# Setup of an eight-batch gated cross-attention kernel taken apart: loads in order of need on two queues, whole fills of ones, constants as steps of the first batch, later weights in the loop

## The chip, the cores and the metric

The kernel runs on one core of a Trainium2 chip. The metric is the device time of one execution in microseconds (us), lower is better. Engines: PE multiplies matrices, DVE, ACT and POOL work on vectors, SP only issues transfers (DMA). Each engine runs its own list of instructions in order and waits on semaphores that others raise. DMAs are issued by an engine's queue and flow on 16 shared DMA engines.

## The reference

Input x is 8 batches of 256 rows by 128 features, with a context of the same shape. Four layers follow each other. Each adds, behind a tanh gate, an attention with 16 heads of 8 features (queries from the layer-normed x, keys and values from the context), and then, behind another gate, a feed-forward part of the layer-normed x:

```python
x = x + tanh(g_xattn[l]) * attention_l(layernorm(x), ctx, ctx)
x = x + tanh(g_ffn[l]) * ffn_l(layernorm(x))
```

Layer 2's attention is causal, layer 3's keeps for each head only the 51 queries of 256 that lie best on the keys. The feed-forward parts: layer 0 routes 3 rows in 4 through a 128x128 block with gelu; layer 1 is a mixture of 8 experts (best 2 of 8) plus a shared one, with silu; layer 2 the same with hidden width 512 and gelu; layer 3 rounds x and the weight w3 to a six-bit grid in blocks of 32 and multiplies them.

## The kernel before, in words

The work of one batch is a fixed list of some 260 small steps (`stream_steps`, L73): `keys`, `stats`, `norm`, `turn`, `query`, `maxima` (scores and their row maxima), `max_parts`, `max_turn`, `attend` and `weigh` (scores again, turned, exponential, product with the values), `heads`, `project`, and the feed-forward steps. Four batches are in flight in four slots; batch b + 4 takes the slot of batch b. In which order the batches take turns is written out by hand as digits in `TURNS_TAKEN` (L120); `SCHEDULE` (L152) is the resulting list of 2144 (step, batch, layer, part). Every engine walks the same list and issues its own part of each step, so its queue has the order of the list, and an engine that waits in one step holds back all later ones. `signals` (L155) tells how often each step raises which semaphore, and the wait values are counted from it.

Scores come from stacked tiles: `k_st` and `q_st` hold, for each pair of heads, keys and queries split into three bf16 terms. ACT writes the first term (L573) and a copy (L578), POOL makes the other two (L517 to L522), and SP scatters them with six DMAs per `keys` (L468) and six per `query` (L477) into every eighth row of the stack. One row in 32 of `k_st` holds ones and the same row of `q_st` the negated row maxima, which `max_turn` moves there by one SP DMA of 16 KB (L481); PE's first `attend` of that batch and layer waits for it (L789). After the last `attend`, `max_clear` (L485) copies a row of zeros of `k_st` over the maxima.

Before the loop stands the setup:

- SP (L434 to L447) issues w3, then the 14 `attention_loads` (L385), then context and x of four slots.
- DVE (L882 to L970) clears slot 0 (`clear`, L416: `q_st` to zero, two small fills, `k_st` to zero), writes the rows of ones one by one (`set_ones`, L423), quantises w3 in 14 parts (`fp6`, L898), waits for all attention loads, makes bf16 and gated copies of constants, splits the weights of all layers (L953), and at last fills `junk` and raises `setup_done` (L970).
- POOL (L499 to L508) clears slots 1 to 3, writes their twelve rows of ones (L426), issues six `ffn_loads` and seven `big_loads` (two of 2 MB each), and waits for `setup_done`.
- ACT (L552 to L556) and PE (L641 to L645) wait for the loads, turn the quantised w3, and wait for `setup_done`.

In the loop, POOL's `norm` makes h (L527, L531) and behind it, for the attention norms, adds the gated output bias `gbo` to x (L539), which raises `xb_ready`; SP's next load of x and DVE's `project` wait for that.

Of the kernel before, what the change touches and what calls it, by code (L numbers as in the profile page):

```python
# [12 lines left out]
P = 128  # L13
# [16 lines left out]
CBANKS = 2  # L30
VR = HD + 1
# [41 lines left out]
def stream_steps():  # L73
# [6 lines left out]
    for l in range(LAYERS):  # L80
        out += norm(l) + [("turn", l, 0), ("query", l, 0)] + [("load_x", 0, 0)] * (l == 0)
# [5 lines left out]
        out += tiles + [("max_parts", l, 0), ("max_parts", l, 1), ("max_turn", l, 0)]  # L87
# [33 lines left out]
0000101011033112132200302000000201301213101001001001001120201200200210021121031211210312021312030011  # L121
0131231231010122101220101000212020122003223023311030221111122132131312122223010030320122333203323032
0230230310323212303203103200010320123103100103100001313332003230103031032011331011121121021123032220
0120000001110102023223213210231112012023223213212312201213113102230212011320032011112002110002321013
2201222222311332112101221331230303102321230300020322232302210013022013203100033103011310302130012131
2112113021031322213011233301100211020221010223301220312211100120203022103030212000103030110110210032
1230002213301223303021111222002220311023300322101220013131001102123211312113022222013222100201001302
3111021012023021201202202132203020212103311333010120000010000120031301000133001010103010203032220332
3010302231332300013211202110111233113313111220212101111101313101301320103131022031031132303313030000
0323310222112210203414141122113222112131341142421133122214152534343545234534345522432422344323332254  # L130
5523453542445445245424542534523434342343543544523345424245443523553543534445355544354425435245534243
2533453425235342332325532353232256655565563453545663444454434636453536456336433644346436443364333646
4563445345436353465446653364363336453666433434636635466366534436543653666346475474477464446566575646
4564676456546547645566457575755765767554757575754754546767476545476457547764767765746556576555775756
5556755566577557665555756746656747564574646744466746656677775764656664654475446757456776654666666574
4666446766756664566645756666546647557557567567575577745547554447465746477677677644776776675644447547
5654756566745475567455677576747656467665775474474476576475477477466464574777476746774557754477757477
5446475766545666555766647547546564754765647576667765556654746554575664566447566476574474747747747767
6447475764765445567544455676554565465655556757764447774476754556464776465744455757457677747576775774
7755775466746657667677776657766746754647664677765455557455455767455564666546666646645664665466757667  # L140
7767567564765756777776757466764677745757774575747574775757746767577757677757567776757647675456767676
76746464767747576767675675767467675674476677
# [12 lines left out]
def signals(step, b, l, part):  # L155
# [3 lines left out]
        "load_x": {},  # L159
        "load_ctx": {},  # L160
# [5 lines left out]
        "norm": {f"h_ready{s}": 1, "xb_ready": int(l < LAYERS or l == 2 * LAYERS - 1)},  # L166
# [7 lines left out]
        "max_parts": {"m_parts_done": part},  # L174
# [92 lines left out]
def flamingo(nc, x, ctxT, attn_w, bias_cols, bias_rows, g_all, router0, block0, router1, fc1, fc2,  # L267
             gate_up, down, router2, w1, ws1, b1_cols, w2, ws2, b2_all, w3, ident_in, causal_qk,
             causal_kq, before_in, iota_in, out):
    with ExitStack() as ctx:  # L270
# [10 lines left out]
        def sem(name):  # L281
# [92 lines left out]
        w3_loaded, cleared, attn_loaded, ffn_loaded, big_loaded = sem("w3_loaded"), sem("cleared"), sem("attn_loaded"), sem("ffn_loaded"), sem("big_loaded")  # L374
        zeroed_first, zeroed = sem("zeroed_first"), sem("zeroed")
        gates_done, w3_quantised, w3_turned = sem("gates_done"), sem("w3_quantised"), sem("w3_turned")
        w3_copied, setup_done, setup_step = sem("w3_copied"), sem("setup_done"), sem("setup_step")
# [7 lines left out]
        attention_loads = [  # L385
            (wqk_in.rearrange("d l j n -> d l (j n)"), attn_w[:, :, 0:2, :].rearrange("d l j n -> d l (j n)")),
            (wvo[:, :, :, :].rearrange("d l j n -> d l (j n)"), attn_w[:, :, 2:4, :].rearrange("d l j n -> d l (j n)")),
            (bcol[0:HALF, :, :], bias_cols.rearrange("(m a) l c -> a m l c", a=2)[0, :, :, :]),
            (bcol[HALF:P, :, :], bias_cols.rearrange("(m a) l c -> a m l c", a=2)[1, :, :, :]),
            (ident[:, :], ident_in), (bv_all[:, :], bias_rows[:, R_BV:R_BO].broadcast_to([P, LAYERS * D])),  # L390
            (rows_in, bias_rows[:, R_BO:R_GB].broadcast_to([P, R_GB - R_BO])),
            (gate_b[:, :], bias_rows[:, R_GB:R_GB + EXPERTS].broadcast_to([P, EXPERTS])), (gates[:, :], g_all.broadcast_to([P, 2 * LAYERS])),
            (cqk, causal_qk), (ckq, causal_kq), (iota[:, :], iota_in),
            (before_f, before_in), (r0_sb[:, :], router0)]
# [983 lines left out]
```

## Time and profile before

| | us |
|---|---|
| median of 3 runs | 1045.1 (1043.42 to 1047.93) |
| profiled execution | 1045.38, its span 1043.6 |
| busy PE / DVE / ACT / POOL | 920.3 / 784.0 / 608.0 / 407.3 |
| mean granted PE clock | 0.954 |

The span runs from the first instruction to the last; the execution's own time is 1.8 us longer. Busy time is the sum of the durations of an engine's instructions; what lies between is idle. `A <-B` behind a row names what ended an idle time.

### The profile page before, as it was taken

To read this page: it belongs to the slowest core of one execution; us is meant where nothing else is said; L and a number is where in the kernel's file an instruction comes from. 1 tells how busy PE (TensorE), PEld (TensorE's weight loads), DVE (VectorE), ACT (ScalarE), POOL (GpSimd) and SP (SyncE) were. 2 spreads that over 40 slices of the span, in tenths; PEclk is the share of its full clock that TensorE was granted. 3 is DMA by queue.
4 is the path that set the end of the run, shared out by engine and by line. 5 is a ranking of instruction groups with operands and counts; after the bars stand their busy time and mean duration, and the time that the engine had idled before them with its cause. 6 is when DMAs were issued, how large, how long until landed. Compare 5 with 4: busy or idle time off the path is not lost.

```text
span 1043.6 us, 22358 instructions
## 1 busy us (share of the span) xinstructions
PE 920.3 (88%) x7921; PEld 606.1 (58%) x7921; DVE 784.0 (75%) x2688; ACT 608.0 (58%) x1301; POOL 407.3 (39%) x481
## 2 busy tenths in 40 slices
PE   0379789999999999889986799999999999999883
PEld 0224345665589888357633355556469987767522
DVE  7289999887655455997898999888946456656787
ACT  0147667445675544778674575655685457786641
POOL 9812533224244113464346144333460333252322
PEclk9769999999999999999998899999999999999956
DMA  6921211101010000002112111111010010010000
GB/s 182 283 62 30 57 35 33 32 17 46 6 43 21 17 16 17 19 23 53 26 28 60 26 37 49 33 33 32 19 48 2 17 32 16 3 32 1 19 2 22
DMA packets 67037, 39.91 MB, mean 38 GB/s; under 512 B 7911, under 2 KB 64768, under 8 KB 66928
## 3 DMA queue, kind: packets, MB, share of 16 engines
q1 hardware_dynamic: 65008, 31.70, 11.9%
q0 software_dynamic: 1920, 6.78, 2.1%
q8 instruction: 66, 1.08, 0.5%
q14 instruction: 43, 0.35, 0.1%
HBM read 11.19 MB, written 1.05 MB: 12 GB/s over the span
## 4 chain that ended last, share of the span: by engine, by line
PE 70%; DVE 13%; POOL 7%; ACT 5%; issue 3%; DMA 1%; SPq 1%; ACTq 0%; POOLq 0%; DVEq 0%
PE A L867 12%; PE B L858 11%; PE C L713 9%; PE A L827 6%; PE A L674 6%; DVE mx L1166 6%; PE B L693 6%; PE A L837 3%; PE A L660 3%; ACT probs L592 3%; POOL h L531 3%; PE B L653 2%; PE A L798 2%; PE B L700 2%; PE B L749 2%
## 5 line engine op out<-in xcount | busy, mean ns | idle before, releaser
L1166 DVE TENSOR_REDUCE mx<-A 128x2 f32<-128x512 f32 (+1 forms) x480 | 306.4, 683 | 51.4 <-PE A L674 35.1
L592 ACT ACTIVATE probs<-B 128x512 f32<-128x512 f32 (+1 forms) x512 | 264.5, 570 | 98.5 <-PE B L693 63.6
L527 POOL TENSOR_TENSOR rstd<-veps,mhalf 128x2 f32<-128x2 f32 x64 | 47.4, 741 | 359.5 <-DVE veps L1126 359.0
L632 ACT ACTIVATE probs<-B,b_sb 128x256 f32<-128x256 f32 x288 | 118.8, 472 | 87.5 <-PE B L858 85.9
L713 PE MATMUL C<-probs,v_aug 128*9 128x256 f32 (+1 forms) x2048 | 153.6, 380 | 2.6 <-ACT probs L592 2.5
L1089 DVE SCALAR_TENSOR_TENSOR xs<-A,comb,xs 128x128 f32<-128x128 f32 x272 | 82.4, 345 | 97.2 <-PE A L867 75.7
L867 PE MATMUL A<-w_sb,probs 128*128 128x128 f32 x1152 | 141.1, 277 | 0.1
L867 PEld LDWEIGHTS A<-w_sb,probs 128*128 128x128 f32 x1152 | 135.9, 192 | 5.7 <-issue 2.9
L858 PE MATMUL B<-hT,w_sb 128*128 128x256 f32 x576 | 138.3, 384 | 0.0
L674 PE MATMUL A<-k_st,q_st 64*128 64x256 bf16 (+1 forms) x1024 | 100.4, 279 | 39.6 <-DVE mx L1166 27.2
L545 POOL TENSOR_TENSOR rn<-ss,mhalf 128x32 f32<-128x32 f32 x16 | 88.0, 5502 | 119.1 <-DVE ss L1013 119.1
L858 PEld LDWEIGHTS B<-hT,w_sb 128*128 128x128 f32 x576 | 104.2, 190 | 16.6 <-issue 2.3
L693 PE MATMUL B<-q_st,k_st 64*128 64x256 bf16 (+1 forms) x1024 | 99.7, 272 | 10.5 <-ACT probs L592 7.5
L674 PEld LDWEIGHTS A<-k_st,q_st 64*128 64x128 bf16 x1024 | 34.6, 95 | 105.4 <-DVE mx L1166 66.7
L531 POOL TENSOR_SCALAR h<-xs,mv,rstd 128x128 f32<-128x128 f32 x112 | 90.4, 814 | 5.8
L563 ACT ACTIVATE hT<-B 128x256 f32<-128x256 f32 x96 | 37.0, 387 | 90.2 <-PE B L653 89.7
L693 PEld LDWEIGHTS B<-q_st,k_st 64*128 64x128 bf16 x1024 | 35.1, 95 | 74.8 <-ACT probs L592 42.5
L827 PE MATMUL A<-hT,fc_sb 128*128 128x256 f32 x320 | 78.3, 387 | 0.0
L713 PEld LDWEIGHTS C<-probs,v_aug 128*9 128x9 f32 x2048 | 34.2, 89 | 56.2 <-issue 22.2
L517 POOL TENSOR_TENSOR resid<-resid,q_parts 128x256 f32<-128x256 f32 x32 | 22.0, 686 | 107.3 <-ACT resid L578 107.3
L827 PEld LDWEIGHTS A<-hT,fc_sb 128*128 128x128 f32 x320 | 56.8, 190 | 11.3 <-issue 2.1
L621 ACT ACTIVATE probs<-A 128x256 f32<-128x256 f32 x80 | 30.5, 385 | 51.9 <-PE A L827 51.5
(196 smaller groups left out, 1396.6 us busy)
## 6 DMA issues: line engine op xcount, KB each, us to landing
k_st<-k_parts SPq DMA_DIRECT2D x192, 64.0 KB, 2.0
q_st<-q_parts SPq DMA_DIRECT2D x192, 64.0 KB, 2.1
w_sb<-in_w POOLq DMA_DIRECT2D x2, 2048.0 KB, 14.9
cT<-in_ctxT SPq DMA_DIRECT2D x8, 128.0 KB, 2.7
x_in<-in_x SPq DMA_DIRECT2D x8, 128.0 KB, 3.3
fc_sb<-in_fc POOLq DMA_DIRECT2D x1, 1024.0 KB, 6.2
out_x<-xs SPq DMA_DIRECT2D x8, 128.0 KB, 1.8
probs<-in_attn_w SPq DMA_DIRECT2D x1, 512.0 KB, 4.3
```

Of the source, the lines that this page charges most:

```text
L531: ins = nc.gpsimd.tensor_scalar(h[s][:, r, :], (x_in if l == 0 else xs)[s][:, r, :], mv[s][:, r, 0:1], rstd[s][:, r:r + 1], ALU.subtract, ...
L545: nc.gpsimd.tensor_tensor(rn[s][:, :], ss[s][:, :], mhalf[:, :], ALU.pow)\
L592: nc.scalar.activation(probs[s][:, part % UNIT_RING, 2 * a:2 * a + 2, 0:n], b_bank(w, a + 1)[:, 0:2 * n].rearrange("p (j q) -> p j q", j=2 ...
L632: ins = nc.scalar.activation(hid[s][:, part % UNIT_RING, c, :], b_bank(w, half + 1)[:, j * ROWS:(j + 1) * ROWS], ACT.Gelu, bias=b1_sb[:, p ...
L674: ins = nc.tensor.matmul(a_bank(w, a + 1)[:, i * keys:(i + 1) * keys], head_rows(q_st, s, a, hp0 + i, r * P, P), head_rows(k_st, s, a, hp0 ...
L693: ins = nc.tensor.matmul(b_bank(w, a + 1)[:, j * n:(j + 1) * n], head_rows(k_st, s, a, 2 * g + j, t * P, P), head_rows(q_st, s, a, 2 * g + ...
L713: ins = nc.tensor.matmul(C[VW * i:VW * i + VR, C_BANK[b, l, u // 4], g % 2, q0:ROWS], v_aug[s][:, t, 4 * g + i, :], probs[s][:, u % UNIT_R ...
L827: ins = nc.tensor.matmul(a_bank(w, k + 1)[:, a * ROWS:(a + 1) * ROWS], fc1_sb[:, 2 * part + k, a, :], hT[s][:, :], start=True, stop=True)
L858: ins = nc.tensor.matmul(b_bank(w, half + 1)[:, j * ROWS:(j + 1) * ROWS], w1_sb[:, part, 2 * half + j, :], hT[s][:, :], start=True, stop=True)
L867: ins = nc.tensor.matmul(a_bank(w, 1)[:, r * D:(r + 1) * D], hid[s][:, part % UNIT_RING, c, r * P:(r + 1) * P], w2_sb[:, part, c, :], star ...
L1089: ins = nc.vector.scalar_tensor_tensor(xs[s][:, r, :], a_bank(w, 1)[:, r * D:(r + 1) * D], scale(r), xs[s][:, r, :], ALU.mult, ALU.add)
L1166: nc.vector.tensor_reduce(mx[s][:, r, a, hp0:hp0 + n], a_bank(w, a + 1).rearrange("p (n k) -> p n k", n=n), AX.X, ALU.max).then_inc(sems[" ...
```

## The change

The step list of a batch gets three steps in layer 0: `setup` parts 0 and 1 behind `query`, and part 2 behind `max_turn`; they do something for batch 0 alone. `load_x` moves from behind `query` to behind `max_parts` part 0. `TURNS_TAKEN` is written anew: leaving `setup` and `load_x` out, both lists have the same 2136 steps, in an order that differs in 437 places, by 5 steps or fewer for most. The first steps are now keys, stats, stats, norm of batch 0, keys 1, turn 0, stats 1, stats 1, norm 1, query 0, turn 1, setup part 0, keys 3, keys 2, stats 3, query 1, stats 2, stats 3, setup part 1, stats 2, maxima 0; `setup` part 2 is the 40th step; batch 0's `heads`, at which POOL issues the big loads, is the 86th; batch 1's `max_turn` and first `attend` are the 69th and the 78th.

Loads and clearing:

```diff
+        first_loads = [
+            (wqk_in[:, 0, :, :], attn_w[:, 0, 0:2, :]),
+            (bcol[0:HALF, :, :], ...), (bcol[HALF:P, :, :], ...),
+            (wvo[:, 0, :, :], attn_w[:, 0, 2:4, :]), (ident[:, :], ident_in),
+            (bv_all[:, :], bias_rows[:, R_BV:R_BO].broadcast_to([P, LAYERS * D]))]
+        gate_loads = [(gates[:, :], g_all.broadcast_to([P, 2 * LAYERS]))]
+        attention_loads = [
+            (rows_in, ...), (gate_b[:, :], ...), (iota[:, :], iota_in), (r0_sb[:, :], router0),
+            (wqk_in[:, 1:LAYERS, :, :] ...), (wvo[:, 1:LAYERS, :, :] ...),
+            (cqk, causal_qk), (ckq, causal_kq), (before_f, before_in), (w3_sb, w3)]
 ...
-        def clear(engine, s, zeroed):
+        def clear(engine, s, cleared):
 ...
-            engine.memset(k_st[s][:, :, :].bitcast(F32), 0.0).then_inc(zeroed, 1)
-        def set_ones(engine, s):
-            for row in range(0, P, HALF // MAX_TERMS):
-                ins = engine.memset(k_st[s][row:row + 1, :, :].bitcast(U32), TWO_ONES)
-            return ins
+            engine.memset(k_st[s][:, :, :].bitcast(U32), TWO_ONES).then_inc(cleared, 1)
```

SP, which waits in `keys` of the first four batches for its slot's clearing (DVE clears slots 0 and 1, POOL 2 and 3):

```diff
-            sp.dma_start(w3_sb, w3).then_inc(w3_loaded, 16)
-            for dst, src in attention_loads:
-                sp.dma_start(dst, src).then_inc(attn_loaded, 16)
-            for s in range(SLOTS):
+            for i, (dst, src) in enumerate(first_loads):
+                sp.dma_start(dst, src).then_inc(first_loaded, 16)
+                if i == 0:
+                    load_ctx(0, 0)
+                if i == 2:
+                    load_x(0, 0)
+            for s in range(1, SLOTS):
                 load_ctx(s, s)
                 load_x(s, s)
 ...
-                    sp.dma_start(q_st[s][0:P:HALF // MAX_TERMS, :, :], k_st[s][BLK - 1:P:HALF // MAX_TERMS, :, :])\
+                    sp.dma_start(q_st[s][0:P:HALF // MAX_TERMS, :, :], q_st[s][BLK - 1:P:HALF // MAX_TERMS, :, :])\
```

POOL:

```diff
-            for s in range(1, SLOTS):
-                clear(nc.gpsimd, s, zeroed)
-            pool.wait_ge(zeroed, SLOTS - 1)
-            for s in range(1, SLOTS):
-                set_ones(nc.gpsimd, s).then_inc(cleared, 1)
-            for dst, src in ffn_loads: ...
-            for dst, src in big_loads: ...
-            pool.wait_ge(setup_done, 1)
+            for s in range(DVE_SLOTS, SLOTS):
+                clear(nc.gpsimd, s, cleared_pool)
 ...
+                if step == "setup" and b == 0 and part == 2:
+                    for dst, src in ffn_loads: ...
+                if step == "heads" and b == 0 and l == 0:
+                    for dst, src in big_loads: ...
-                if step == "norm" and (l < LAYERS or l == 2 * LAYERS - 1):
+                if (step == "max_parts" and part == 0) or (step == "norm" and l == 2 * LAYERS - 1):
+                    if not set_up:
+                        pool.wait_ge(setup_done, 1)
 ...
                     nc.gpsimd.tensor_tensor(xs[s][:, :, :], (x_in if l == 0 else xs)[s][:, :, :],
```

ACT issues the gates and the first four attention loads before the loop, and the other six in the first `keys`; it waits for `setup_done` only at the first `attend`. PE waits for it at the first `max_turn`:

```diff
-            act.wait_ge(attn_loaded, 16 * len(attention_loads))
+            for dst, src in gate_loads: ...
+            for dst, src in attention_loads[:EARLY_LOADS]: ...
 ...
+                if step == "keys" and (b, l) == (0, 0):
+                    for dst, src in attention_loads[EARLY_LOADS:]: ...
+                if step == "setup" and b == 0 and part == 2:
+                    copy_ac(1, w3T[:, :], b_bank(w, 1)[:, 0:D])
 ...
-            pe.wait_ge(w3_quantised, 1)
-            pe.wait_ge(attn_loaded, 16 * len(attention_loads))
-            nc.tensor.transpose(B[:, 0, 0:D], work_rows[0][0][:, 0, :], ident[:, :]).then_inc(w3_turned, 1)
-            pe.wait_ge(w3_copied, 1)
-            pe.wait_ge(setup_done, 1)
+            pe.wait_ge(first_loaded, 16 * len(first_loads))
+            pe.wait_ge(first_ready, 1)
 ...
+                if step == "setup" and b == 0 and part == 2:
+                    pe.wait_ge(w3_quantised, 1)
+                    pe.wait_ge(sems["b_read"], w.free("b_read", 1))
+                    nc.tensor.transpose(b_bank(w, 1)[:, 0:D], work_rows[0][0][:, 0, :], ident[:, :]).then_inc(sems["b_full"], 1)
```

DVE, where `split_heads(l)` is the pair of copies of L953 and `set_up()` holds the other constants, as before but for their order:

```diff
+            dve.wait_ge(first_loaded, 16 * len(first_loads))
+            split_heads(0).then_inc(first_ready, 1)
+            dve.wait_ge(cleared_pool, SLOTS - DVE_SLOTS)
 ...
+                if step == "setup" and b == 0 and part == 0:
+                    set_up()          # first waits for attn_loaded and gates_done
+                if step == "setup" and b == 0 and part == 1:
+                    for n in range(FP6_PARTS):
+                        ins = fp6(n, 0, 1, w3_sb.unsqueeze(1), work_rows[0][0][:, 0:1, :])
 ...
+                    ins.then_inc(w3_quantised, 1)
+                    nc.vector.memset(junk[:, :, :], 0.0).then_inc(setup_done, 1)
```

## Rows read from the trace of the kernel before

**Rows 1.** Busy time by stretch: length, busy us (count) by engine, PEclk, DMA share, GB/s.
```profile
0.00:24.00 24.00, 0.50 (x2) 0.24 (x2) 20.70 (x56) 1.77 (x3) 22.96 (x36) 1.00 0.58 167
...
40.00:50.00 10.00, 3.37 (x10) 2.48 (x10) 2.09 (x11) 2.06 (x5) 8.87 (x14) 0.74 1.14 249
...
60.00:70.00 10.00, 8.94 (x50) 3.30 (x50) 8.60 (x16) 4.54 (x11) 3.43 (x6) 0.50 0.12 30
```

**Rows 2.** Chain that ended last, opening: start us, us, what.
```profile
17.81 0.95 POOL k_st L426
...
28.86 0.67 POOL resid L517
...
33.21 0.72 POOL xs L539
...
42.04 8.00 DMA q_st<-q_parts
```

**Rows 3.** Timeline of the opening: start us, us, engine line operation tile.
```profile
2.59 1.27 SPq L436 DMA_DIRECT2D bcol<-in_bias_cols  x2
...
4.53 0.43 SPq L436 DMA_DIRECT2D bv_all<-in_bias_rows  x1
...
8.06 0.29 DVE L903 TENSOR_REDUCE amax<-probs 128x4 f32<-128x128 f32 x1
...
14.83 0.76 DVE L941 CAST identb<-ident 128x128 bf16<-128x128 f32 x1
...
15.57 1.05 DVE L943 CAST ckq_b<-probs 128x128 bf16<-128x128 f32 x1
...
19.82 1.52 DVE L953 COPY wqk<-probs 128x128 f32<-128x128 f32 x8
...
23.38 0.48 DVE L970 MEMSET junk<- 128x512 f32 x1 [0.17 <-DVE gbo L965]
...
23.97 1.19 PE L725 MATMUL B<-cT,wqk 128*128 128x256 f32 x2 [8.53 <-DVE junk L970]
...
25.64 0.47 ACT L578 ACTIVATE resid<-B,bcol 128x256 f32<-128x256 f32 x1
...
26.05 0.42 DVE L1099 TENSOR_TENSOR v_aug<-A,bv_all 128x256 f32<-128x256 f32 x1 [2.19 <-PE A L660]
...
27.19 0.78 DVE L1126 TENSOR_SCALAR veps<-mv 128x2 f32<-128x2 f32 x1
...
50.72 1.29 DVE L1166 TENSOR_REDUCE mx<-A 128x2 f32<-128x512 f32 x2 [3.82 <-PE A L674]
```

**Rows 4.** Timelines of POOL, SP and PE around batch 1's first attend.
```profile
69.17 0.67 POOL L522 TENSOR_TENSOR q_parts<-resid,q_parts 128x256 bf16<-128x256 f32 x1
...
76.89 0.59 SPq L481 DMA_DIRECT2D q_st<-mT  x1
...
79.22 0.40 PE L693 MATMUL B<-q_st,k_st 64*128 64x256 bf16 x4
```

**Rows 5.** DMA issues, several stretches: count, KB each, median us to landing.
```profile
bv_all<-in_bias_rows SPq DMA_DIRECT2D x1, 256.0 KB, 3.9
...
w_sb<-in_w POOLq DMA_DIRECT2D x1, 2048.0 KB, 11.0
...
k_st<-k_parts SPq DMA_DIRECT2D x1, 64.0 KB, 7.6
...
k_st<-k_parts SPq DMA_DIRECT2D x2, 64.0 KB, 13.5
...
q_st<-q_parts SPq DMA_DIRECT2D x192, 64.0 KB, 2.1
```

**Rows 6.** Busy time by stretch, where the granted clock changes.
```profile
30.00:32.00 2.00, 0.00 (x0) 0.00 (x0) 0.00 (x0) 0.00 (x0) 1.82 (x3) 0.79 1.01 370
...
72.00:73.00 1.00, 1.00 (x20) 0.43 (x16) 0.56 (x2) 0.57 (x2) 0.00 (x0) 0.94 0.50 128
```

**Rows 7.** Busy time by stretch, one later dip.
```profile
560.00:570.00 10.00, 5.11 (x37) 2.92 (x36) 9.74 (x41) 3.71 (x10) 6.59 (x10) 0.85 0.41 107
```

More of the change, by code:

```diff
@@ L30 @@
 CBANKS = 2
+DVE_SLOTS = 2
+EARLY_LOADS = 4
 VR = HD + 1
@@ L80, in stream_steps @@
     for l in range(LAYERS):
-        out += norm(l) + [("turn", l, 0), ("query", l, 0)] + [("load_x", 0, 0)] * (l == 0)
+        out += norm(l) + [("turn", l, 0), ("query", l, 0)] + [("setup", 0, 0), ("setup", 0, 1)] * (l == 0)
         tiles = [("maxima", l, part) for part in range(len(MAX_TILES[l]))]
@@ L126 @@
[L126 to L130, printed above, removed]
@@ L159, in signals @@
         "load_x": {},
+        "setup": {"b_full": int((b, part) == (0, 2)), "b_read": int((b, part) == (0, 2))},
         "load_ctx": {},
@@ L461, in _ @@
                 if step == "keys":
+                    if (b < SLOTS) and l == 0:
+                        sp.wait_ge(*cleared(s))
                     for n in range(3):
@@ L586, in _ @@
                     n = ROWS - (P * (part % RT) if l == CAUSAL else 0)
+                    if not set_up:
+                        act.wait_ge(setup_done, 1)
+                        set_up = True
                     if part >= UNIT_RING:
@@ L882, in _, with split_heads @@
             nc.vector.memset(mhalf[:, :], -0.5)
-            nc.vector.memset(mean_k[:, :], 1.0 / ROWS)
-            clear(nc.vector, 0, zeroed_first)
-            dve.wait_ge(zeroed_first, 1)
-            set_ones(nc.vector, 0)
-            setup_count = iter(range(1, 100))
-            def next_setup():
-                return next(setup_count)
+            for s in range(DVE_SLOTS):
+                clear(nc.vector, s, cleared_dve)
+            def split_heads(l):
+                for a in range(2):
+                    ins = nc.vector.tensor_copy(wqk[:, l, :, a * HALF:(a + 1) * HALF],
+                                                wqk_in[:, l, :, :].rearrange("p j (m a) -> p a j m", a=2)[:, a, :, :])
+                return ins
+            dve.wait_ge(first_loaded, 16 * len(first_loads))
+            split_heads(0).then_inc(first_ready, 1)
+            dve.wait_ge(cleared_pool, SLOTS - DVE_SLOTS)
             def blocks(ap):
@@ L949, in _ @@
-            nc.vector.memset(C[:, :, :, :], 0.0)
-            for l in range(LAYERS):
-                for a in range(2):
-                    nc.vector.tensor_copy(wqk[:, l, :, a * HALF:(a + 1) * HALF],
-                                          wqk_in[:, l, :, :].rearrange("p j (m a) -> p a j m", a=2)[:, a, :, :])
-            for c, row in enumerate((R_BQ3, R_BK3)):
-                for a in range(2):
-                    nc.vector.tensor_copy(bqk3[:, c, a * HALF:(a + 1) * HALF],
-                                          rows_in[:, row - R_BO:row - R_BO + D].rearrange("p (m a) -> p a m", a=2)[:, a, :])
```

153 lines of the change are left out of this document (84 added, 69 removed).

## The prediction

> **What bounds the kernel now.** I read the table of busy time by stretch first. DVE is busy for 20.70 of the first 24 us and PE for 0.50; from 40 to 50 us DVE does 2.09 us of work and PE 3.37 [rows 1]. So the opening has two parts: a prologue in which nothing of the loop runs, and then some 25 us in which the loop has begun but neither PE nor DVE has enough to do. The chain of waits says why: POOL's twelve one-row fills of the key tiles run until 18.76 us, then its thirteen weight loads are issued, and only at 28.86 us does POOL do the first split of the loop; later the chain waits 8.00 us for a query transfer to land, at 50.04 us [rows 2]. The timeline gives the dates that the change touches: first loop matmul at 23.97 us, first row maximum on DVE at 50.72 us [rows 3]. After that the two engines fill up, so what is won before the first maximum is won for the whole kernel, unless a new wait gives it back. The profiled execution took 1045.38 us (span 1043.6), the median of the three runs is 1045.1: they differ by 0.3 us, and I take what I save off the median.
>
> **Part 1: the first matmul.** Before, PE, ACT and POOL all wait for all constants. Now PE waits for six loads and two copies on DVE. SP issues one load after another, at 0.43 us (bv_all) to 0.64 (a bias column) each; w3, two big loads, two bias columns and ident stand ahead of bv_all, issued at 4.53 us [rows 3]. In the new order wqk of layer 0, ctx, two bias columns, x, wvo and ident stand ahead of it: seven instead of six, so about 4.9 us. It landed 3.9 us after its issue [rows 5]: 8.8 us. The two splitting copies of layer 0 are a quarter of the eight that took 1.52 us [rows 3], 0.4 us; with a hop, PE starts at 9.3 us, 14.7 us earlier. The clearing is two slots on DVE and two on POOL, four large fills each. With 0.95 us for a fill [rows 2] both are done by 6 us, under the cover of the loads.
>
> **Part 2: queries.** From the first matmul to the end of ACT's second pass it took 2.1 us (23.97 to 26.11) [rows 3], which brings us to 11.4. POOL, no longer held by load issues, then does key split and norm (28.86 to 33.21, 4.35 us [rows 2]), the same for batch 1, and the query split, 1.9 us: 10.6 us, to 22.0, and with small waits 22.5. One more issue, 0.6 us, and a transfer of 2.1 us when nothing disturbs it [rows 5] give queries in place by about 25.5 us. Two such transfers of lag more would make 30. That is 20 to 25 us before 50.04, so this is no longer the last wait.
>
> **Part 3: constants, now the last wait.** DVE does the constants as a loop step standing ahead of the key tiles 3 and 2 and of maxima, and waits there for six loads that ACT issues after its first key pass: 9.3 + 2.1 = 11.4 us, six issues of 0.6 us to 15.0 us. The trace has no DMA issued by ACT; SP's are the nearest (0.43 us to 0.64). ACT's next key pass stands behind these six, which POOL's first norm covers. With landing as for bv_all the last is there at 18.5 us (16.5 if they queue nowhere, 20.5 if key transfers slow them). The constants took from 14.83 to 23.38 us, 8.5 us, of which two copies and waits leave: 8.0 at most [rows 3]. Some of these ran slowly while POOL's fills were running (the cast at 15.57 us took 1.05 us for 128x128, where w3's first operation on as many elements took 0.29). That cover is gone, POOL does splits and norms instead, so I take 7.2 and as the lower end 5.5. Then two value adds, two statistics pairs and one variance chain: 26.05 to 27.97 us is one of each [rows 3], 1.9, and another add and pair, 0.9, make 2.8. Then quantising w3: 6.8 us before (8.06 to 14.83) [rows 3], at 0.29 for each of 17 operations 4.9; POOL is mostly waiting by then, so I take 5.2. The junk fill 0.5 and slot 2's variance chain 0.9. Sum: 18.5 + 7.2 + 2.8 + 5.2 + 0.5 + 0.9 = 35.1 us for DVE's first maximum, against 50.72: **15.5 us won** (12 with all upper ends of DVE work, 10 with late loads too, 20 with all lower ends).
>
> The Trainium skill ("SBUF — State Buffer", section "SBUF: two separate sides") says that DVE in a two-port mode or with two SBUF inputs and GpSimd take a port pair in turn, each holding it for a whole instruction. By it the price of part 3 falls only as far as POOL is idle; the trace's slow operations beside fills agree, and with POOL as busy as before it would be the 12 us of gain.
>
> **Part 4: the smaller moves.** DVE loses four one-row fills, in a stretch where it now waits for loads: nothing further. w3's turn and copy stand in the loop after the first turn of maxima, their input ready: 0.5 us of PE at worst, beside DVE's maxima. POOL's addition of gbo (0.72 us at 33.21 [rows 2]) leaves every attention norm and comes at the maxima: whoever is behind it in POOL's queue is served 0.7 us earlier, and the projection needs it much later. I count 0 (0 to 1 won). The six ffn loads now cost POOL about 4 us in the loop, issued at 41 to 45 us; POOL's next work, query 2's split, began two splits of 1.9 us before 69.84 [rows 4], so comes at 66.0 - 15.5 = 50.5: they are covered. Their 2.1 MB are in by about 51.
>
> **Part 5: what is given back.** The seven big loads go from 23 us, where nobody needed a short transfer at once, to POOL's `heads` step of batch 0. POOL waits for nothing between query 3's split, which ended at 69.84 us, and that step [rows 4]: 69.84 - 15.5 = 54.3 us, an addition, three small loads, and the first 2 MB is issued at 56.1 and flies for 11.0 us [rows 5], the second for as long behind it, to about 72. Into it falls the transfer of batch 1's maxima, issued by SP at 76.89 - 15.5 = 61.4 us. PE's first `attend` of batch 1 waits for it, in order, with DVE's further maxima and all else queued behind it on PE. Before, it was issued at 76.89 and PE took it up at 79.22 [rows 4], 2.3 us for a transfer of about 2.0. The nearest row of a short SP transfer beside a 2 MB load is the first key transfer of the loop, with nothing ahead of it in its queue: 7.6 us; with a full queue 13.5 [rows 5]. At 7.6 PE stands still for 7.6 - 2.3 = **5.3 us**; at 2.3 or less for 0, at 13.5 for 11.2. I take 5.3, since query 3's transfers are just being drained.
>
> The Trainium skill ("DMA: Bandwidth & Descriptors", section "Queues, rings and completion order") says that a DMA engine goes round its queues a whole packet at a time. By it a transfer this small (16 KB) waits for one packet's turn at most, anything from 2 us to the 7.6, not for the load's end: the sum would then be 0 to 5.3 us given back. The 13.5 us row is a queue's own backlog under that rule, and no run here shows a 16 KB transfer beside a load.
>
> Then the clock. The granted clock was 0.50, the lower level (1.2 of 2.4 GHz), from 60 to 70 us, with PE 9 tenths busy, and rose in 72 to 73 (0.94); it had fallen in 30 to 32 (0.79), in which PE did nothing [rows 1, 6]. A stall of 5.3 us may bring it down again. If it falls, ten us of dense work at half clock cost 5 us; if DVE is the bound meanwhile, nothing. I take 2.5.
>
> **Sum:** -15.5 + 5.3 + 2.5 = -7.7 us: 1045.1 - 7.7 = 1037.4 us.
>
> **Rivals.**
> A (forecast, 0.42): as above, 1034 to 1041.
> B (0.27): the transfer slips through, or the loads are not yet under way; the stall and the clock loss go. 1045.1 - 15.5 = 1029.6, with the upper ends of DVE work 1033. For it: 16 KB against 64. Against: the 7.6 us row had no backlog either, and query 3's transfers add some.
> C (0.25): nothing gained that can be told. Either the start wins only 10 us (late loads, constants as slow as before) and A's 7.8 comes off: 1042.9; or the new order in which batches take turns, which changes in over 400 places, costs one more stretch like 560 to 570 us (PE 5.11 of 10 busy, clock 0.85 [rows 7]): 5 us, 1042.3. It may as well save one, which A's range holds.
> D (0.06), slower: the maxima's transfer needs 13.5 us behind queries 3 and an x load in its own queue, 11.2 us of stall, and 5 us of half clock: 16.2 against 15.5 won, 1045.8; with a start that wins 10, 1051. It decides once stall and clock loss exceed what the start gains, a landing of over 12.8 us. For it: SP's queue did reach 13.5. Against: it took twelve 64 KB transfers in a row.
>
> **How the numbers follow.** A change below 0.5%, 5.2 us, can't be told from none. Below 1039.9 lie B and most of A: 0.27 + 0.36 = 0.63. Slower than 1050.3 is part of D and of C's tail: 0.05. The rest is 0.32. The range reaches from B's point, 1029.5, to just above D's milder case, 1046.5.
>
> **What would show it.** First loop matmul near 9.3 us, no POOL one-row fills, DVE's set-up copies from about 18.5 us, first maximum at 33 to 38 us on DVE, released by DVE's own order and not by a DMA. The big loads from about 56 us; a PE idle of 4 to 8 us in front of batch 1's first `attend`, released by the transfer of mT, and a granted clock of 0.5 behind it. I am wrong if the first maximum comes after 41 us, if that idle is under 1 us or over 10, or if the later stretches, from 150 us, take over 4 us more or less than before.

## The result, and the profile after

The changed kernel takes 1036.73 us (median of 7 runs, 1033.37 to 1041.97) against 1044.87 us (median of 7 runs of the kernel before on the same chip): a ratio of 0.9923, 95% interval 0.9899 to 0.9948, or 8.1 us less. The forecast was 1037.4. The profiled execution took 1036.73 us (span 1034.9). The total was forecast well, in part by luck, because two errors in its terms nearly cancel: the traces give back 5 to 6 us more than forecast in the first 90 us, and win some 4 us later that the sum had at zero.

**The opening.** Timelines of PE, DVE and POOL of the changed kernel from 4 to 36 us (start in us, duration, engine and line, operation, and in brackets the idle time before it and what ended it). They answer to [rows 2, 3].

```profile
10.31 1.19 PE L746 MATMUL B<-cT,wqk 128*128 128x256 f32 x2 [10.31 <-DVE wqk L917]
```
```profile
9.84 0.36 DVE L917 COPY wqk<-probs 128x128 f32<-128x128 f32 x2 [4.34 <-DMA bv_all<-in_bias_rows]
...
19.45 0.23 DVE L1092 CAST identb<-ident 128x128 bf16<-128x128 f32 x1 [4.33 <-DMA probs<-in_w]
...
24.31 0.41 DVE L1128 TENSOR_TENSOR v_aug<-A,bv_all 128x256 f32<-128x256 f32 x1
...
27.28 0.27 DVE L936 TENSOR_REDUCE amax<-probs 128x4 f32<-128x128 f32 x1
...
28.74 0.64 DVE L944 TENSOR_TENSOR raw<-raw 128x128 f32<-128x128 f32 x1
...
30.77 0.28 DVE L952 TENSOR_TENSOR raw<-raw 128x128 f32<-128x128 f32 x1
...
31.93 0.29 DVE L959 TENSOR_TENSOR raw<-raw 128x128 f32<-128x128 f32 x1
...
33.39 0.48 DVE L1124 MEMSET junk<- 128x512 f32 x1
...
34.16 1.28 DVE L1195 TENSOR_REDUCE mx<-A 128x2 f32<-128x512 f32 x2
```
```profile
28.52 0.72 POOL L520 TENSOR_TENSOR resid<-resid,q_parts 128x256 f32<-128x256 f32 x1
...
30.40 0.77 POOL L530 TENSOR_TENSOR rstd<-veps,mhalf 128x2 f32<-128x2 f32 x1
31.27 1.62 POOL L534 TENSOR_SCALAR h<-x_in,mv,rstd 128x128 f32<-128x128 f32 x2
```

The first maximum has no bracket: DVE came to it from its own queue, and the queries had long been there. It starts at 34.16 us where it was 50.72, 16.6 us earlier. Inside the quantising, the same kind of operation took 0.64 us at 28.74, beside POOL's work on 256 elements a row, 0.28 us at 30.77, beside its work on 2, and 0.29 us at 31.93, beside POOL's `tensor_scalar`, which reads one tensor of SBUF.

**The stall.** Timelines of POOL, SP and PE around batch 1's first attend, and the DMA table of the issues from 57 to 57.5 us and from 57.8 to 58 us (count, KB each, median us to landing). They answer to [rows 4, 5].

```profile
55.80 0.95 POOL L542 DMA_DIRECT2D w_sb<-in_w  x1
...
57.28 1.70 POOL L542 DMA_DIRECT2D w_sb<-in_w  x1
```
```profile
53.97 3.81 SPq L487 DMA_DIRECT2D q_st<-q_parts  x6
57.83 0.69 SPq L441 DMA_DIRECT2D x_in<-in_x  x1
59.11 0.59 SPq L491 DMA_DIRECT2D q_st<-mT  x1
```
```profile
61.17 0.39 PE L695 MATMUL A<-k_st,q_st 64*128 64x256 bf16 x4
72.84 0.61 PE L714 MATMUL B<-q_st,k_st 64*128 64x256 bf16 x4 [11.27 <-DMA q_st<-mT]
```
```profile
q_st<-q_parts SPq DMA_DIRECT2D x2, 64.0 KB, 8.8
...
x_in<-in_x SPq DMA_DIRECT2D x1, 128.0 KB, 12.7
```
```profile
59.11 13.64 DMA q_st<-mT
```

The last line is from the chain of waits: the 16 KB were issued at 59.11 us and released PE 13.64 us later. In the same queue the last query transfers (issued at 57 us) needed 8.8 us and the x load ahead of the maxima (issued at 57.83) 12.7 us. PE stood still for 11.27 us where 5.3 was forecast. The busy times by stretch (length, PE, PEld, DVE, ACT and POOL busy with counts, granted clock, DMA share, GB/s) answer to [rows 1]:

```profile
60.00:70.00 10.00, 1.56 (x20) 0.38 (x16) 2.81 (x5) 1.66 (x4) 0.50 (x1) 0.72 1.00 328
70.00:80.00 10.00, 7.12 (x64) 3.14 (x68) 3.69 (x9) 3.80 (x7) 0.00 (x0) 0.59 0.49 138
80.00:90.00 10.00, 9.27 (x112) 4.30 (x106) 9.85 (x24) 8.50 (x18) 2.45 (x4) 1.00 0.07 18
```

**Landmarks.** The kernel has 32 `project` steps (the attention's product with its output weights, added to x), each one DVE operation, in both programs:

```profile
88.07 0.48 DVE L1203 SCALAR_TENSOR_TENSOR xs<-A,tg,xs 128x256 f32<-128x256 f32 x1
```
```profile
83.53 0.48 DVE L1232 SCALAR_TENSOR_TENSOR xs<-A,tg,xs 128x256 f32<-128x256 f32 x1
```

The first fence is the first of them before, the second after: 88.07 - 83.53 = 4.5 us ahead. Doing this at six of them, for the changed kernel and the experiments below, gives the lead (us) that each has over the kernel before. Each row is one profiled execution, which can differ from its kernel's median (fills_only's took 1035.26 us, its median is 1037.68), so small differences between rows show little. Where the turns differ, the steps between two landmarks differ slightly too.

| lead at (us of before) | 88 | 178 | 552 | 650 | 902 | 1024 |
|---|---|---|---|---|---|---|
| changed kernel | 4.5 | 5.3 | 4.6 | 5.0 | 5.1 | 8.7 |
| m1_on_act | 8.7 | 9.5 | 7.3 | 6.3 | 6.1 | 9.6 |
| big_after_m1 | 17.9 | 11.7 | 9.5 | 7.4 | 7.6 | 11.1 |
| big_pieces | 15.3 | 10.3 | 9.0 | 9.5 | 9.6 | 13.1 |
| pieces_by_norm | 17.5 | 17.0 | 15.3 | 14.7 | 14.8 | 18.4 |
| w3_late | 19.8 | 18.9 | 9.9 | 10.4 | 10.5 | 14.1 |
| old_order | 4.2 | 2.1 | 1.8 | 1.5 | 1.5 | 1.5 |
| xs_in_norm | 4.9 | 2.7 | 0.2 | -0.8 | -0.8 | 2.5 |
| fills_only | 9.9 | 9.5 | 8.8 | 7.5 | 7.4 | 10.1 |
| fills_and_loads | 1.9 | 1.6 | 1.6 | 1.1 | 1.0 | 1.2 |
| new_order_only | 1.9 | -0.1 | -1.1 | -4.3 | -4.4 | -0.2 |

Of a lead of 16.6 us at the first maximum, 17.8 at the turn of batch 1's maxima (58.05 us, was 75.83), 4.5 are left at 88 us: the stall took 11.3, and the 2.0 that remain I put to the half clock behind it (from batch 1's first `attend` to the landmark it took 10.69 us, 72.84 to 83.53, against 8.85, 79.22 to 88.07, before). Later 4.2 come back, 3.6 of them between 902 and 1024 us.

### The profile page after: what moved, and what is told of

Read it like the earlier page. It is cut to its first block, busy times and chain, and to the rows that moved or that the text cites. A ratio compares the mean times of both kernels' runs of the same rounds, so it can differ in the third digit from the quotient of the medians.

```text
span 1034.9 us, 22347 instructions
## 1 busy us (share of the span) xinstructions
PE 917.7 (89%) x7921; PEld 604.8 (58%) x7921; DVE 776.9 (75%) x2688; ACT 606.0 (59%) x1299; POOL 397.4 (38%) x465
## 3 DMA queue, kind: packets, MB, share of 16 engines
q1 hardware_dynamic: 62944, 29.98, 11.2%
HBM read 11.19 MB, written 1.05 MB: 12 GB/s over the span
## 4 chain that ended last, share of the span: by engine, by line
PE 71%; DVE 13%; POOL 6%; ACT 4%; issue 3%; DMA 2%; SPq 0%; ACTq 0%; DVEq 0%
PE B L886 12%; PE A L895 12%; PE C L734 9%; PE A L855 7%; PE A L695 6%; PE B L714 6%; DVE mx L1195 6%; PE A L681 4%; PE A L865 3%; POOL h L534 3%; PE B L674 2%; ACT probs L615 2%; PE A L826 2%; PE B L721 2%; PE B L746 2%
## 5 line engine op out<-in xcount | busy, mean ns | idle before, releaser
L734 PE MATMUL C<-probs,v_aug 128*9 128x256 f32 (+1 forms) x2048 | 151.4, 376 | 1.9 <-ACT probs L615 1.7
L855 PEld LDWEIGHTS A<-hT,fc_sb 128*128 128x128 f32 x320 | 57.0, 190 | 11.2 <-issue 2.3
```

Source lines behind the costliest of these rows:

```text
L734: ins = nc.tensor.matmul(C[VW * i:VW * i + VR, C_BANK[b, l, u // 4], g % 2, q0:ROWS], v_aug[s][:, t, 4 * g + i, :], probs[s][:, u % UNIT_R ...
L855: ins = nc.tensor.matmul(a_bank(w, k + 1)[:, a * ROWS:(a + 1) * ROWS], fc1_sb[:, 2 * part + k, a, :], hT[s][:, :], start=True, stop=True)
```

## The experiments

Each ratio is to the kernel before, run beside it on the same chip, with its 95% interval; 0.001 is 1.04 us. The changed kernel's own is 0.9923. The theory was: the start wins 15 to 17 us, a stall for one short transfer takes most of it, and the order of turns or the place of the `gbo` addition gives the rest. All twelve runs are told here.

### 1. m1_on_act: batch 1's maxima sent from ACT's empty queue

```diff
-                if step == "max_turn":                          # SP
+                if step == "max_turn" and (b, l) != (1, 0):
...
                     copy_ac(1, mT[s][:, :], ...)                # ACT
+                    if (b, l) == (1, 0):
+                        act.wait_ge(sems["b_read"], w.at("b_read", 1))
+                        act.dma_start(q_st[s][0:P:HALF // MAX_TERMS, :, :], mT[s][:, :])...
```

> The changed kernel, but batch 1's maxima of layer 0 (16 KB) are sent by ACT's queue, which has nothing else in it, at the same place of the order. Theory L (the 2 MB loads on POOL's queue hold up every other queue's transfers): the landing stays long, 6 to 13 us, PE idles 4 to 11 us before batch 1's first attend, time 1032 to 1037. Theory Q (SP's own queue was the delay: query transfers and a 128 KB x load ahead of the 16 KB): lands in 2 to 3 us, PE idles under 1 us there, and with it the half clock goes: 1037 - 11 - 2 = 1024.

1034.36 us, ratio 0.9884 (0.9862 to 0.9906). Timelines of ACT and PE:

```profile
61.64 1.13 ACTq L607 DMA_DIRECT2D q_st<-mT  x1
```
```profile
68.56 0.61 PE L717 MATMUL B<-q_st,k_st 64*128 64x256 bf16 x4 [3.62 <-DMA q_st<-mT]
```

The same loads are in flight, but PE goes on 6.9 us after the issue instead of 13.7 and waits 3.6 us instead of 11.3. The 7.7 us between the two waits are not all won: 4.3 are an earlier release (68.56 us, was 72.84), and 3.4 come from PE reaching this `attend` later. The first maximum starts 1.0 us later (35.20) and PE stays at the lower clock to 56.87 us instead of 50.84 (granted 0.65 against 0.96 from 50 to 60 us). The 4.3 are what shows at the landmark at 88 us (8.7 against 4.5).

Neither theory holds alone: the loads keep even a transfer with nothing ahead of it for 6.9 us, and SP's own backlog doubles that. The issue is 2.5 us later here, but that doesn't explain the shorter landing. Counted from the issue of the second 2 MB load, the maxima landed 15.5 us on in the changed kernel, 13.3 in old_order, 15.1 in fills_and_loads and 15.6 (batch 2's) in big_after_m1, all from SP's queue, and 10.2 us on here, from ACT's. No run separates the query transfers' part of the backlog from the x load's.

### 2. big_after_m1: POOL issues the large loads only when those maxima have landed

```diff
                 if step == "heads" and b == 0 and l == 0:
+                    pool.wait_ge(sems["m_moved1"], 16)
                     for dst, src in big_loads:
```

> The changed kernel, but POOL waits until batch 1's maxima have landed before it issues the seven big loads. L: the idle of 11.3 us before batch 1's first attend is gone (under 1 us), the loads fly from about 62 to 78 us and meet batch 2's maxima and layer 1's first key transfers, of which the worse one costs 0 to 8 us: 1024 to 1032. Q: the same idle goes, and nothing comes in its place, since there is no row of queries in SP's queue by then: 1024.

1033.01 us, 0.9867 (0.9843 to 0.9891), a microsecond slower than the slower end of either theory. The lead at 88 us is 17.9: without this stall the whole start is kept. But the next transfer of maxima, batch 2's, now falls into the loads:

```profile
71.83 0.55 SPq L491 DMA_DIRECT2D q_st<-mT  x1
```
```profile
79.99 0.61 PE L715 MATMUL B<-q_st,k_st 64*128 64x256 bf16 x4 [4.96 <-DMA q_st<-mT]
```

Ahead of this transfer in SP's queue is only an x load, issued 4.3 us before it (67.53 us), and it still needed 8.07 us. The lead is down to 11.7 by 137 us. Whole loads issued 7 us later moved the stall, they did not remove it; no run issues them whole where the loop has long been dense.

### 3. big_pieces: the large loads in sixteen pieces of 256 KB, one per weigh step

```diff
+                if step == "weigh" and l == 0 and b in (1, 2, 3) and pieces_left:
+                    pool.wait_ge(sems["pv_done"], w.at("pv_done", 1))
+                    dst, src = pieces_left.pop(0)
+                    pool.dma_start(dst, src).then_inc(big_loaded, 16)
```

> The changed kernel, but the two 2 MB loads are sixteen of 256 KB, and POOL issues one of the 21 pieces behind each weigh step of batches 1 to 3 in layer 0 instead of all at heads. L: no transfer waits longer than some 3 us for a piece, the idle before batch 1's first attend is under 1.5 us, the clock stays at 1.0 there, and the time is 1037 - 11 - 2 = 1024 (1021 to 1028). A third theory, T, that PE or DVE are bound later anyway and catch up, says that the time won at 60 us is lost again by 300 us: 1033 or more.

The five smaller of the big loads go the same way, 21 issues in all. 1031.22 us, 0.9856 (0.9838 to 0.9874), where 1024 was expected. No wait for a transfer of maxima is left, though the pieces fly from 65 us on. But POOL works in order, and a piece that waits for a weigh step holds up what is behind it, so they came in bursts ahead of POOL's norms. POOL's timeline, then PE's waits from 88 to 110 us (total, times, longest):

```profile
90.73 1.86 POOL L550 DMA_DIRECT2D w_sb<-in_w  x3
92.61 0.74 POOL L537 TENSOR_TENSOR rstd<-veps,mhalf 128x2 f32<-128x2 f32 x1
```
```profile
PE B L682 <- POOL h L541: 3.8, 2, 2.7
```

Of the kernel before the same waits for h are 1.1 us. The lead goes from 15.3 at 88 us to 10.3 at 137.

### 4. old_order: the changed kernel with the turns of before

```diff
-SCHEDULE = schedule()
+SCHEDULE = old_order()     # batches take turns as before; setup steps where they must stand
```

> The changed kernel with the turns of the kernel before (setup steps put in at the same neighbours, load_x behind max_parts). Theory O (part of the gain is the new order: before to after won another 3 us at the end, 1000 to 1024 us): 1039 to 1041. Theory N (the order is neutral, the end varies from run to run): within 2 us of the changed kernel's 1037.

1045.32 us (10 runs), 0.9998 (0.9979 to 1.0017), slower than either theory had it. The order of turns, which the forecast had at zero, is worth 0.0075 in the changed kernel, 7.8 us, with some 3 us to either side. PE's waits from 24 to 100 us:

```profile
PE B L756 <- DMA q_st<-mT: 9.1, 1, 9.1
PE B L716 <- POOL h L576: 6.2, 2, 5.1
```

The stall is 2.2 us shorter than in the changed kernel, but the first maximum starts at 37.05 us (2.9 later), and 6.2 us of waits for POOL's norms are there, of which the changed kernel has 1.1. At 88 us the two are level (4.2 and 4.5). In the leads the order's worth lies behind that: 2.9 us between 88 and 178, and 3.6 between 902 and 1024, where old_order wins nothing.

### 5. fills_only: the kernel before, with key tiles filled whole

```diff
-            engine.memset(k_st[s][:, :, :].bitcast(F32), 0.0)
+            engine.memset(k_st[s][:, :, :].bitcast(U32), TWO_ONES)
...
-                set_ones(nc.gpsimd, s).then_inc(cleared, 1)     # and DVE's
...
-                    sp.dma_start(q_st[...], k_st[s][BLK - 1:P:..., :, :])
+                    sp.dma_start(q_st[...], q_st[s][BLK - 1:P:..., :, :])
```

> The kernel before, with one edit of the change: key tiles filled with ones whole, no row fills, and max_clear's zeros from the query tile. POOL's 11.7 us of row fills go, so its loads are issued from 6.7 us instead of 18.7, its first split is at about 23.5 us (setup_done, then ACT) instead of 28.9. Theory S (the start is a chain, what goes from its front goes from its end): 4 to 6 us won, with the query transfer's landing of 8 us shorter as well since the big loads fly earlier: 1036 to 1041. Theory P (the prologue as a whole has to go, DVE's constants keep PE out until 19 us anyway, and POOL's issues meet the first loads in flight): under 3 us, 1042 to 1045.

1037.68 us (5 runs), 0.9939 (0.9913 to 0.9965): 6.4 us by the ratio, 7.3 by the medians, which can't be told from the whole change. Its start is slower than the change's (first loop matmul at 21.82 us, first maximum at 42.31), but its large loads are issued ahead of the loop, no wait for a transfer of maxima is left, and the granted clock stays up. Two stretches of it:

```profile
24.00:60.00 36.00, 20.60 (x94) 10.07 (x94) 20.88 (x54) 8.41 (x21) 24.35 (x38) 1.00 0.64 168
60.00:70.00 10.00, 9.30 (x129) 3.30 (x125) 9.86 (x18) 8.77 (x18) 1.26 (x3) 1.00 0.30 79
```

The changed kernel has a granted clock of 0.68 in the first of these and, as shown, 0.72 in the second.

### 6. fills_and_loads: fills_only, and the later loads of the change

```diff
-            for dst, src in ffn_loads: ...      # POOL, ahead of the loop
-            for dst, src in big_loads: ...
+                if step == "max_turn" and b == 0 and l == 0: ...   # ffn_loads, in the loop
+                if step == "heads" and b == 0 and l == 0: ...      # big_loads, in the loop
```

> The kernel before with the whole fills and with the ffn loads at max_turn and the big loads at heads of batch 0, as the change has them; constants still in a prologue, old turns. S: loop starts at 19 to 20 us instead of 24, maxima at about 36 instead of 50.7; then the stall before batch 1's first attend, 6 to 12 us as in the changed kernel, and its half clock: net 1 to 6 us won at 88 us. Whatever is left there stays to the end, since the order is the old one: 1040 to 1045.

1045.8 us (10 runs), 1.0011 (0.9992 to 1.003). The first maximum is 4.3 us earlier than in fills_only (37.98 us), and all is lost again, 0.8 us past the upper end of what was expected:

```profile
75.10 0.61 PE L692 MATMUL B<-q_st,k_st 64*128 64x256 bf16 x4 [6.98 <-DMA q_st<-mT]
```
```profile
70.00:80.00 10.00, 4.90 (x39) 1.78 (x40) 2.10 (x4) 3.04 (x6) 0.00 (x0) 0.54 0.77 220
```

So the later loads, the very part that frees the start, cost 7.5 us against fills_only. Here the x load was issued 4.6 us ahead of the maxima (61.06 and 65.67 us) instead of 1.3, and they needed 9.34 us to land.

### 7. new_order_only: the kernel before with the new turns

```diff
-TURNS_TAKEN = (of before)
+TURNS_TAKEN = (of the change), setup steps left out
```

> The kernel before, whole prologue and all, with only the turns of the change (setup steps do nothing, load_x behind max_parts). Theory O (the order itself is worth what the changed kernel has over the same kernel with the old turns, 1045.3 to 1036.7): 5 to 8 us faster, 1037 to 1040. Theory F (the new turns only fit the new start; with the old prologue they are worth nothing): within 2 us of 1045.

1044.92 us (12 runs), 0.9998 (0.9984 to 1.0011): nothing. The table says why it is nothing: it is 4.4 us behind at 902 us and wins 4.2 after. The stretch between the landmarks at 901.96 and 1018.22 us, with the old turns (kernel before), then with the new turns (this kernel), with nearly the same work in both (871 and 868 matmuls, 337 and 334 operations on DVE):

```profile
901.96:1018.22 116.26, 106.56 (x871) 68.29 (x871) 82.08 (x337) 76.87 (x148) 40.23 (x32) 0.88 0.05 12
```
```profile
906.34:1018.61 112.27, 102.44 (x868) 66.37 (x868) 80.28 (x334) 76.51 (x147) 40.54 (x32) 0.92 0.05 13
```

It is 4.0 us shorter, at a granted clock of 0.92 instead of 0.88. Whether the clock is the cause is not shown. The changed kernel has the same stretch:

```profile
896.85:1009.73 112.88, 102.57 (x867) 66.42 (x866) 81.09 (x333) 76.52 (x147) 41.19 (x33) 0.92 0.05 13
```

### 8. pieces_by_norm: the changed kernel, pieces one by one behind POOL's own work

```diff
+                if step in ("norm", "keys", "query") and w.i >= STEP["norm", 1, 1, 0] and pieces_left:
+                    dst, src = pieces_left.pop(0)
+                    pool.dma_start(dst, src).then_inc(big_loaded, 16)
```

The three small loads stay at `heads`; the others, in eighteen pieces, follow from batch 1's second layer on, one behind each of these steps, with no wait of their own.

> The changed kernel with the big loads in eighteen pieces, one behind each of POOL's norm, keys and query steps from batch 1's layer-1 norm on (about 170 us), where PE is the bound. Theory L: the 15 us by which the first pieces kernel led at 88 us are kept, none is lost between 88 and 137 us, where pieces in front of POOL's norms cost 3 to 5: 1027 (1025 to 1030). Theory T (later stretches take back what the start wins): 1031 or more.

1026.44 us (5 runs, 1024.25 to 1027.09), 0.9817 (0.9795 to 0.984): the fastest of all, with an interval clear of the kernel before and of the changed kernel (0.9899 to 0.9948). The stretch of the old stall:

```profile
60.00:70.00 10.00, 9.55 (x120) 3.95 (x113) 9.56 (x19) 8.14 (x17) 0.00 (x0) 1.00 0.07 19
```

PE is busy for 9.55 of 10 us where the changed kernel had 1.56. The lead of 17.5 us at 88 us is 14.8 at 902, and the last stretch brings it to 18.4, as in every kernel with the new turns. The pieces are also later than the whole loads (the first is issued at 101.42 us, where about 170 was expected, the last at 202.30), so this run alone doesn't say whether size or date keeps them harmless. In experiment 3 pieces of the same size beside the first layer left no wait for maxima, where whole loads did (2): that speaks for size.

### 9. w3_late: pieces_by_norm, with w3 quantised and turned in the loop

```diff
+W3_AT = (("norm", 1, 5, 0), ("norm", 2, 5, 0))    # its two setup steps stand ahead of these
+SCHEDULE = w3_later()
```

It also loads w3 to a tile of its own, fills `junk` with the other constants and issues the ffn loads at batch 0's `max_turn`.

> The pieces_by_norm kernel, with w3 loaded to a tile of its own and quantised (and turned) not in front of the first maxima but near 300 us, where DVE is busy for two thirds of the time. Theory D (the first maximum waits for DVE's constants, and DVE stays the bound until 200 us): the first maximum comes 5 to 6.5 us earlier, at 28 to 29 us, just behind the query transfers, and the gain stays: 1026.4 - 5.5 = 1021 (1019 to 1023). Rival R (the order was written for the later start; what is won in front turns into waits for transfers or h): under 2 us won, 1025 or more.

1034.35 us, 0.991 (0.9893 to 0.9928). That is slower than both theories, whose point was 1021. The start did what it should: first maximum at 29.81 us, 4.6 earlier, lead 19.8. Then DVE ran the 17 operations in one piece, 162.73 to 169.7 us, and PE, which had been full, waited for the work behind them:

```profile
163.03 0.61 PE L708 MATMUL A<-wvo,cT 128*128 128x128 f32 x4
163.56 0.62 PE L761 MATMUL C<-probs,v_aug 128*9 128x256 f32 x8
170.85 1.19 PE L892 MATMUL A<-fc_sb,probs 128*128 128x128 f32 x4 [6.66 <-DVE probs L1347]
```
```profile
165.74 0.59 DVE L987 TENSOR_SCALAR junk<-junk 128x128 f32<-128x128 f32 x1
166.25 0.75 DVE L988 TENSOR_TENSOR junk<-junk 128x128 f32<-128x128 f32 x1
...
169.63 0.74 DVE L1342 SCALAR_TENSOR_TENSOR probs<-probs,A 128x256 f32<-128x256 f32 x2
```

The lead falls from 18.9 to 10.5, more than was won. The steps were meant for a place near 300 us, where DVE is idle for a third of the time (busy 13.28 of 20 us from 280 to 300), but the place chosen is reached at 163 us. DVE was busy 8.95 of the 10 us before 160: there was no idle time to put 7 us of work into. So the run shows what a full engine costs; the place that was meant stays untested.

### 10. xs_in_norm: the changed kernel, the gbo addition back in the norm

```diff
-        "norm": {..., "xb_ready": int(l == 2 * LAYERS - 1)},
+        "norm": {..., "xb_ready": int(l == 2 * LAYERS - 1 or (l < LAYERS and not early(b, l)))},
+def early(b, l): return l == 0 and b < SLOTS     # there gbo isn't ready, it stays at max_parts
```

> The changed kernel, but POOL's addition of gbo to x stays in norm, behind h, as in the kernel before, except for the first four batches' layer 0, where it would wait for the setup. Theory X (the new turns need POOL free of this 0.72 us behind each h; the new order alone lost 2 us between 88 and 155 us and 3 more at 650): 3 to 7 us slower than the changed kernel, 1040 to 1044. Theory Y (the addition's place is worth nothing, as the prediction had it): within 2 us of 1036.7.

1041.51 us (12 runs), 0.9971 (0.9953 to 0.9988). The stall is the same (11.4 us). The lead at 88 us is 4.9 and then melts to -0.8. The place of this addition, which the forecast had at zero, is worth 0.9971 - 0.9923 = 0.0048 here, about 5 us, with some 3 us to either side. By the edit above the first four batches keep the addition at `max_parts` in layer 0; the 5 us are for all the others. The leads drift apart from 88 to 902 us, at no single place.

### 11. new_order_xs: the kernel before, with the new turns and the addition moved

```diff
 new_order_only, and
-        "norm": {..., "xb_ready": int(l < LAYERS or l == 2 * LAYERS - 1)},
+        "norm": {..., "xb_ready": int(l == 2 * LAYERS - 1)},
+        "max_parts": {..., "xb_ready": int(part == 0)},
```

> The kernel before with two edits of the change: the new turns, and the addition of gbo at max_parts; the whole prologue stays. X: the two together win 5 to 8 us, 1037 to 1040, though the new turns alone won nothing. Y: 1043 to 1046.

1044.6 us (12 runs), 1.001 (0.9997 to 1.0022). With the old start, both together win nothing. So the two alone do not make up the missing microseconds.

### 12. xs_only: the kernel before, with the addition and the x loads moved

```diff
 the edits of new_order_xs without the new turns; load_x behind max_parts
```

> The kernel before with the addition of gbo (and load_x) at max_parts, old turns. X: little, 1042 to 1045, since the old turns were written for the addition in norm. Y: 1044 to 1046.

1047.85 us (10 runs), 1.003 (1.0015 to 1.0046): 3.4 us slower on the medians, and above both theories. Alone and on the old turns, the move costs.

## Why the prediction was right, and where it was not

**Part 1 was right within a microsecond.** The first matmul came at 10.31 us instead of 9.3. The term that was off is bv_all's landing: issued at 4.52 us (forecast 4.9), it took 5.30 us and not 3.9.

**Part 2 was right.** The queries had landed by 27.4 us (forecast 25.5, at most 30) and were not the last wait.

**Part 3 was right in its mechanism and to about a microsecond in its sum**, 16.6 us won against 15.5. (Its cautious ends were added up wrongly: by its own terms the upper ends of DVE's work give 13.2 us won and late loads too 11.2, not 12 and 10. The forecast doesn't rest on them.) The constants ran from 19.45 (forecast 18.5) to 24.31 us, 4.9 us where I had taken 7.2 and a lower end of 5.5: four casts and copies of 128x128 took 0.22 to 0.23 us each where the nearest rows of before had 0.76 and 1.05 beside POOL's fills [rows 3]. Then the quantising took 6.1 us, not 5.2. POOL was working, not waiting, and three of DVE's operations with two inputs took 0.63 to 0.65 us beside its `tensor_tensor`. The Trainium skill ("SBUF — State Buffer", section "Who interferes with whom") says that a DVE instruction with two SBUF inputs contends with a GpSimd instruction that reads SBUF. The prediction gave the rule without its condition that GpSimd (POOL) reads. The rows agree in part. In the kernel before, seven of the nine operations with two inputs of the quantising took 0.29 us beside POOL's fills, which read nothing, while casts and one-input operations there took up to 1.06. In the changed kernel such an operation took 0.64 us at 28.74 beside POOL's `tensor_tensor` with two long SBUF inputs. But one took 0.28 us at 30.77 beside a `tensor_tensor` of 0.77 us on two elements a row, and another 0.29 us at 31.93 beside a `tensor_scalar` that reads a whole row. So here it was not every reading instruction of POOL, nor the whole recorded length of one, that held DVE up.

**Part 4 is where two zeros were wrong.** Of the new order it says "It may as well save one", of the addition "I count 0 (0 to 1 won)": taking either back costs the changed kernel 7.8 us (experiment 4) and 5 us (10), each with some 3 us to either side. By the leads the order's worth lies between 88 and 178 us and in the last stretches, there at a better granted clock (7). On the kernel before, neither order nor addition nor both win anything (7, 11, 12). So these are not terms that can be added up: order and place of the addition pay with the changed kernel's start and not with the old one. Why they do is not settled; no run takes the later stretches apart, and none has the new turns on fills_only, which has an earlier start and no stall.

**Part 5 is the step that failed in size.** The mechanism and the place were right, the dates within 2.3 us (maxima issued at 59.11 us, forecast 61.4): big loads from 55.8 us (56.1 forecast), PE's idle in front of batch 1's first `attend`, clock 0.5 behind it. The stall was 11.3 us, not 5.3. "I take 5.3, since query 3's transfers are just being drained" was the wrong choice between the rows: they were not drained, 64 KB transfers issued at 57 us themselves took 8.8 us beside the loads, and the x load of 128 KB ahead of the maxima 12.7. (An x load stood there before too, 2.95 us ahead of the maxima; now it is 1.28 us ahead.) For a transfer with nothing ahead of it the price was about right: 7.6 us taken, 6.9 measured (1). What was taken at nothing is the queue in front of it. It is the 11.2 us that rival D named, with its reason, a queue's own backlog. I said that I am wrong if that idle is over 10 us, and in this term I was. The Trainium skill ("DMA: Bandwidth & Descriptors", section "Queues, rings and completion order") says that a DMA engine goes round its queues a packet at a time. From it the prediction had 0 to 5.3 us of stall, and experiment 1, with ACT's queue empty, lies in that range with 3.6; that it was a packet's turn which took the 6.9 us no run shows. Nothing in it speaks against 13.6 us in a queue that holds other packets, and the two should have been weighed together.

The clock loss was near the forecast (about 2.0, as a remainder, for 2.5). So the sum to 88 us should have been 17.8 - 11.3 - 2.0 = 4.5 and not 7.7, and the total came out by the 4.2 us after it, which is luck. B was out, the transfer did not slip through. C's two reasons were wrong: the start won all it should, and the order gained. Rival D did not decide, since the start had won 16.6 to 17.8 and half clock cost 2.0 and not 5. The bound on the later stretches, over 4 us from 150 us on, was just kept (from 5.3 at 155 us to 8.7).

## What to carry to other kernels

A set-up on the path is worth taking apart, but look for the one cheap edit first: here the whole fills alone gave nearly all of the change's gain, and the rest of the new start paid only once the big loads were out of its way (experiment 8). When bulk loads move into a running loop, ask what else is in the queues at that time, of the short transfer and of all that stands ahead of it in its own queue; whole loads started a little later moved the stall (experiment 2), small and later pieces behind the issuing engine's own steps removed it (8), and pieces that wait on another engine made a new one (3). And work may be moved out of the start only to where the receiving engine is idle in the trace: on a full engine it cost its whole length and more (9).

## What the runs showed of the hardware that I had not expected

A 16 KB transfer needed 13.6 us in SP's queue behind query and x transfers, and 6.9 us in ACT's empty queue, beside the same two loads of 2 MB; the 64 KB transfers of the loop take 2.1 us in the median [rows 5]. Issuing it on ACT cost 1.13 us of ACT's queue at 61.64, where six loads in the opening cost 0.39 to 0.59 us each. And the granted clock can stay at 1.00 through a sparse opening: in fills_only PE was busy for 20.60 of 36 us at a mean of 1.00, in the changed kernel for 20.93 of 36 us at 0.68 (where the same work keeps it busy for longer):

```profile
24.00:60.00 36.00, 20.93 (x171) 8.23 (x171) 32.27 (x73) 12.26 (x28) 25.50 (x39) 0.68 0.49 133
```

No run separates what keeps it up.
